# Last pair: turned output taken out ahead of f_down's product, residual ahead of two gate pairs; first round: next tile's rank product ahead of the turn

## The reference, cut to what matters

```python
x = L0_attn_x
xn = _layernorm(x, axis=-1)
s = _L0_attn_ref(xn, ...)         # RWKV-6: rank mix, r k v g w, state recurrence, group norm, gate, W_o
g = _silu(_L0_ffn_ref(xn, ...))   # silu(xn Wg) * (xn Wu), 2 of each 4 kept, times w_down (f_down)
x = x + s * g
xn = _layernorm(x, axis=-1)
s = _L1_attn_ref(xn, ...)         # Mamba-2 style: dt, B, C, X, scores in chunks of 32, states
g = _silu(_L1_ffn_ref(xn, ...))   # silu(xn Wg) * (xn Wu), times w_down (n_down)
x = x + s * g
# in _L0_attn_ref, the part that is moved:
xxx = x + xx * time_maa_x
a = jnp.tanh(xxx @ time_maa_w1).reshape(B, T, 5, D)
return yn * g @ W_o.T             # yn: normalised and scaled, turned to channels first by PE
```

## Time and profile before

| | us |
|---|---|
| median of three runs | 716.09 |
| lowest and highest | 715.89, 716.32 |
| the profiled execution | 717.52 |
| its span | 715.7 |
| PE busy with matmuls | 702.5 (98%) |
| DVE busy | 496.1 (69%) |
| ACT busy | 338.1 (47%) |
| POOL busy | 76.7 (11%) |

### The profile page before, as it was taken

One profiled execution on the slowest core, in us unless ns is written; L12 is line 12 of the kernel. 1 busy time (PEld: TensorE's weight loads), 2 busy tenths in 40 slices (PEclk: granted clock), 3 DMA queues, 4 the chain that ended last, 5 costly groups with the idle time before them and its releaser, 6 DMA issues.

```text
span 715.7 us, 18156 instructions
## 1 busy us (share of the span) xinstructions
PE 702.5 (98%) x7010; PEld 597.9 (84%) x7010; DVE 496.1 (69%) x1214; ACT 338.1 (47%) x671; POOL 76.7 (11%) x85
## 2 busy tenths in 40 slices
PE   7999999999999999999999999999999999999998
PEld 5777788888888788887888878888788888888887
DVE  5995988528884488755896568954789529895133
ACT  1423782147711586206852068421783237821790
POOL 6301011101110011100111001110011100110020
PEclk9999999999999999999999999999999999999999
DMA  7911460125501364012720236202370025601370
GB/s 231 408 44 30 136 103 18 22 82 143 96 2 30 102 128 83 16 30 89 149 61 16 52 120 110 47 15 74 104 128 23 16 77 136 105 12 25 122 120 16
DMA packets 139572, 59.46 MB, mean 83 GB/s; under 512 B 119728, under 2 KB 131312, under 8 KB 137968
## 3 DMA queue, kind: packets, MB, share of 16 engines
q1 hardware_dynamic: 139504, 58.44, 33.9%
HBM read 44.18 MB, written 14.24 MB: 82 GB/s over the span
## 4 chain that ended last, share of the span: by engine, by line
PE 87%; DVE 5%; issue 3%; DMA 2%; ACT 2%; SPq 1%; POOL 0%; DVEq 0%; POOLq 0%; ACTq 0%
PE psum L1542 68%; PE psum L1651 2%; PE psum L1763 2%; PE psum L1778 2%; ACT BC L626 1%; PE psum L1596 1%; PE psum L1621 1%; PE psum L1816 1%; PE psum L2002 1%; PE psum L1684 1%; PE psum L1863 1%; PE psum L1633 1%; PE psum L1789 1%; PE psum L1735 1%; PE psum L1724 1%
## 5 line engine op out<-in xcount | busy, mean ns | idle before, releaser
L626 ACT ACTIVATE BC<-psum 64x256 f32<-64x256 f32 x128 | 81.6, 637 | 1.9 <-PE psum L1542 0.2
L1542 PE MATMUL psum<-xn1T,sb_n_gate 128*128 128x256 f32 x256 | 61.3, 382 | 0.0
L1542 PE MATMUL psum<-xn1T,sb_n_up 128*128 128x256 f32 x256 | 60.5, 379 | 0.0
L1542 PE MATMUL psum<-xnT,sb_f_gate 128*128 128x256 f32 x240 | 57.8, 383 | 0.0
L1542 PE MATMUL psum<-xnT,sb_f_up 128*128 128x256 f32 x240 | 57.0, 379 | 0.0
L1542 PEld LDWEIGHTS psum<-xn1T,sb_n_gate 128*128 128x128 f32 x256 | 48.0, 190 | 6.8
L1542 PEld LDWEIGHTS psum<-xn1T,sb_n_up 128*128 128x128 f32 x256 | 48.2, 190 | 6.3
L757 ACT ACTIVATE thFB<-psum 128x512 f32<-128x512 f32 x8 | 4.8, 597 | 102.1 <-PE psum L1542 102.1
L1542 PEld LDWEIGHTS psum<-xnT,sb_f_up 128*128 128x128 f32 x240 | 45.2, 189 | 6.8 <-issue 0.3
L1542 PEld LDWEIGHTS psum<-xnT,sb_f_gate 128*128 128x128 f32 x240 | 44.7, 189 | 7.2 <-DVE xnT L1205 0.2
L1542 PE MATMUL psum<-sb_n_down,hidB 128*128 128x256 f32 x224 | 49.5, 379 | 0.0
(11 more groups left out here) (265 smaller groups left out, 1494.4 us busy)
## 6 DMA issues: line engine op xcount, KB each, us to landing
cs_row<-cs_dram SPq DMA_DIRECT2D x8, 1024.0 KB, 5.0
x_dram<-gate SPq DMA_DIRECT2D x8, 512.0 KB, 2.8
cs_half<-cs_dram SPq DMA_DIRECT2D x16, 256.0 KB, 5.8
hidB<-x_dram SPq DMA_DIRECT2D x8, 512.0 KB, 5.7
b_dram<-B_turned SPq DMA_DIRECT2D x32, 128.0 KB, 3.5
hidB<-b_dram SPq DMA_DIRECT2D x8, 512.0 KB, 4.2
X<-in_x SPq DMA_DIRECT2D x9, 256.0 KB, 2.9
XT<-in_x_turned SPq DMA_DIRECT2D x8, 256.0 KB, 2.9
```

The lines of the kernel that those rows point to most:

```text
L626: ins = a_.activation(cols[:, par, 2 * pair:2 * pair + 2, :], src[64 * par:64 * par + 64, :, s, :], ACT.Identity)
L1542: ins = t_.matmul(ps(t, name)[first_row:first_row + rows, col:col + n], w, x, start=(k == 0), stop=(k == len(ws) - 1))
```

## The change

In the last pair alone, ACT does `ffn_tanh(b, "n2", ...)`, `out_scaled` and `ffn_tanh_0` in this order, which were in the opposite order; DVE does `residual_0` ahead of `hidden_n(b, 2)` and `normed_1` ahead of `hidden_n(b, 3)`; PE does `out_0` ahead of `up_n(b, 2)`. At the end of the first round, DVE does `rank_inputs` ahead of `normed_1`, and PE the rank product of the next tile (`rank_first`, which was the first part of `rank_mix`) ahead of `turned_1`. In the first round `kept_busy` does 34 small products and not 39. At the start of PE's program, 40 instructions that only raise `passed` are put between the five identity products and the wait for the first tile.

```diff
@@ ACT, one(a, b), pairs @@
-                    ffn_tanh_0()
-                    out_scaled()
-                    ffn_tanh(b, "n2", thB[0], None, "n0")
+                    if a.reg is not None:
+                        ffn_tanh_0()
+                        out_scaled()
+                        ffn_tanh(b, "n2", thB[0], None, "n0")
+                    else:
+                        ffn_tanh(b, "n2", thB[0], None, "n0")
+                        out_scaled()
+                        ffn_tanh_0()
@@ DVE, one(a, b), pairs @@
-                    hidden_n(b, 2)
-                    residual_0()
-                    hidden_n(b, 3)
-                    normed_1()
+                    if a.reg is not None:
+                        hidden_n(b, 2)
+                        residual_0()
+                        hidden_n(b, 3)
+                        normed_1()
+                    else:
+                        residual_0()
+                        hidden_n(b, 2)
+                        normed_1()
+                        hidden_n(b, 3)
@@ DVE, one(a, b), first round @@
                     differences(a.next())
+                    rank_inputs(a.next())
                     normed_1()
-                    rank_inputs(a.next())
@@ PE @@
+                def rank_first(t):
+                    pe.wait_ge(xxx_ready, t.count(1, 1))
+                    loaded(t.first, "mix", 4)
+                    w1 = packed("w_mix1", NMIX * DMIX)
+                    open_bank(t, "a")
+                    for h in range(CH):
+                        t_.matmul(ps(t, "a")[:, 0:T], w1(h, 0, P), xxxT[:, h, :], start=(h == 0), stop=(h == CH - 1))
+
                 def rank_mix():
-                    pe.wait_ge(xxx_ready, a.count(1, 1))
-                    loaded(first_a, "mix", 4)
                     w1 = packed("w_mix1", NMIX * DMIX)
-                    open_bank(a, "a")
-                    for h in range(CH):
-                        t_.matmul(ps(a, "a")[:, 0:T], w1(h, 0, P), xxxT[:, h, :], start=(h == 0), stop=(h == CH - 1))
+                    if not first_b:
+                        rank_first(a)
@@ PE, last pair @@
                         close_bank(down_part(a, 1, 4, 8), a, "F0")
+                        out_0()
                         up_n(b, 2)
-                        out_0()
                         gate_n(b, 3)
@@ PE, first round @@
-                    kept_busy(["mix_w", "mix_k"], 39)
+                    kept_busy(["mix_w", "mix_k"], 34)
...
                     ffn_p(a.next(), 1)
+                    rank_first(a.next())
                     turned_1()
@@ PE, start @@
                 t_.matmul(ps(Tile(None, 0, first=True), "xT")[:, 0:T], ident[:, :], xnT[:, 0, 1:T + 1], start=True, stop=True)
+
+            for _ in range(40):
+                pe.sem_inc(passed, 1)
             pe.wait_ge(xn_ready, 1)
```

## The result

The changed kernel takes **720.53 us** (median of 4 runs, 718.03 to 721.72), the kernel before 716.21 in the same series (715.89 to 716.42): ratio 1.005, 95% interval 1.0029 to 1.0072. It is 4.3 us slower. The forecast was 716.7, in a range that ended at 718.9.

A forecast was written before the change was run, and what follows sets the result against it. PE, busy 98% of the span, was taken as the bound. +1.55 - 0.16 + 0 - 0.76 = +0.63 gave 718.15 on the profiled execution; the median, 1.43 lower, 716.7 us, range 715.0 to 718.9.

The forecast's parts named there:

- the cause that decided: Rival at the start: PE idles before the first turn and works on at half rate; +2.1 us, 718.8, chance 0.22.
- Steps: Start: 40 semaphore instructions at 0.150 us each delay the first tile's turn to 9.03; 1.55 us later, bounds 1.45 and 1.8.
- Small products: Start, first round: 5 fewer small products ahead of the rank product give 0.16 us back, bounds 0 and 0.16.
- Turn into the first pair: End of first round: idle is filled, but the rank product was already hidden beside ACT's copy; 0, bounds -0.1 and +0.2.
- Last pair: Last pair and step into the drain: out_0 waits less, the xn1T wait goes; 0.76 us back, bounds 0.5 and 0.95.
- Start: Start of PE's program: the 40 steps delay the turn and the whole first round by 1.55 us, none of it hidden.
- The rival's own test: Sign of the slow-start rival (chance 0.22): first half product takes over 1.5 us for its four passes.
- The rival's price: Slow start at half rate: half of a slow stretch of 4.6 us, less a little hidden; +2.1, 718.8, chance 0.22.
- The middle moves: Rival in six middle pairs: PE's instructions shift by 20 places; 0.2 us a pair, -1.2 or +1.2, chance 0.04 each way.

The follow-up runs named there:

- its own kernel: Kernel before with the last pair's three edits and nothing else; 716.71 us, ratio 0.999.
- the kernels with 0.37, 0.64 and 0.95: Seven identity products and 40 steps: on the kernel before, 732.01 us; on the changed kernel with 32 small products, 717.54; on the kernel before with 27, 717.86.
- the kernel with six identity products: Changed kernel with six identity products for five and 33 small products for 34, same instruction count; 719.35 us, ratio 1.0028.
- the 20-step version: Changed kernel with 20 steps for 40 and its small products back from 34 to 39, same instruction count; 715.77 us, ratio 0.9984.
- seven identity products: Changed kernel with seven identity products for five and 32 small products for 34, same instruction count; 717.54 us, ratio 1.0012.
- the kernel with seven products and 40 steps: Kernel before with the 40 steps and seven identity products for five, 48 more instructions; 732.01 us, ratio 1.0201.
- the kernel with 51 small products: Kernel before with 51 small products for 39 in the first round and nothing else, 48 more instructions; 728.8 us, ratio 1.0167.

## Why the prediction was wrong

It named the cause that decided and put it second, at 0.22 and with too small a price. Point by point:

- **Steps, +1.55: right.** First step at 2.8, last at 8.8, turn at 9.03. The Trainium skill (Advanced Engine Details and Errata, DMA Bandwidth Details) puts a semaphore increment at about one cycle; by that rule the turn would have stayed at 7.5. The rows decide against it for an increment that is an instruction of its own: 0.15 a step, 40 times.
- **Small products, -0.16: right in size at full rate**, 0.03 each: twelve fewer gave 0.35 (+1.07 to +0.72), twelve more cost 0.35. In the changed kernel itself the 34 ran at the lower clock, 2.11 where the 39 before took 1.36.
- **Turn into the first pair, 0: right** within its bounds, +0.13.
- **Last pair, -0.76: right**, 0.69 and 0.70 in two profiles, 0.6 in the median of its own kernel, by the steps that were given.
- **The failed step: "Start", that a delay of 1.55 costs 1.55.** The steps do not only delay the turn, they leave the array idle between the identity products and the turn. The forecast took the rate to be full from the first half product on, "as before", because 4.63 us of products come first in both. What stood in front was the same; what stood between was 1.65 us and not 0.10. After idles of 1.65 (twice), 1.72, 1.93 and 1.97 the half product's four passes took 1.82 to 2.08; after 0.16, 0.37, 0.64, 0.80 and 0.95, 1.13. The steps themselves and the late turn are not the cause, since the kernels with 0.37, 0.64 and 0.95 have both; nor does the length of the work ahead tell the two apart: behind 3.88 us of it and 0.80 of idle the passes were fast, behind 4.64 and 1.65 slow. The rival's own test, "over 1.5 us for its four passes", came out true.
- **The rival's price, +2.1:** it took half of one slow stretch of 4.6. By before's product at 20.14 the five slow profiles lay behind by 1.06, the delay as the traces have it, and by 1.3, 1.4 (the changed kernel's), 3.1, 4.2 and 4.2 more, and the two groups of the kernel with six identity products are 4.5 apart. The slow stretch ends earlier or later in each execution, up to past 18 us; a range that ended at 718.9 had room for the two mildest alone.
- **"The middle moves", 0.2 a pair:** not so for this kernel (+20), as the 20-step version shows. But its size was far off as a mechanism: +48 instructions cost 1 to 2 us in each pair. That the changed kernel was spared was luck; nothing in the forecast had priced what its position does.

The loss in three steps: the 20-step version is 0.9 under before; the delay brings it up by 1.77; and from seven identity products to the changed kernel itself the clock adds 3.2 (0.87 to 4.04 above before, across two series). That these make the measured +4.0 is no check, since each step is a difference of the same medians. The check is in the sizes: 1.77 beside 1.48 to 1.74 in the traces, and 3.2 between the 1.3 and 4.2 that the slow profiles lost to the clock.

What stays open: by what the position of the instructions acts. The page counts 57 packets of instructions in q8, 0.93 MB or 16 KB each, about one for every 256 of PE's 14,545 instructions, and the waits recur in each pair at the same two places. In the kernel with seven products and 40 steps no packet starts inside a wait, but one starts 1.1 to 1.9 us ahead of each of the 14 waits at line 1542, and PE goes on 2.2 to 2.9 us behind its start; in the kernel with 51 small products, all 14 again, 1.4 to 2.2 us ahead. A fetch of instructions that comes late would look so. It is likely and not shown: other packets have no wait behind them, in the kernel before too, and no run separated this from another cause. Also open is what happens to the clock between 0.95 and 1.65 us of idle, and whether the faster six executions of the kernel with six identity products had a shorter idle than the slower.

## What to carry to other kernels

A gap ahead of the first real product can cost more than its length, as 1.65 us did here and 0.95 did not: price it also with the work behind it at half rate, and shorten it or put array work into it (two more products won 3 us here). When a change adds or removes instructions ahead of a long unrolled stream, try it also with the count balanced elsewhere, since 48 that took 0.35 us themselves cost 12 us here and would be taken for the change's own. And list all executions with their times and clocks beside any profile: two groups in one kernel show the mechanism better than a median.

## What the runs showed of the hardware that was not expected

- After 1.65 to 1.97 us of idle behind 4.3 to 4.6 us of products, TensorE went at half rate for some 4 to 10 us in five profiles (granted clock 0.50 to 0.55 from 10.3 to 14.1 in four of them); after 0.95 or less it did not. One kernel did either, 6 executions to 6, 4.5 us apart.
- The Trainium skill (TensorE: Matmul & The Clock Gate, What's actually happening) has the slow rate as the default that activity lifts. The trace agrees, and adds that the lift is soon lost: in the changed kernel the turn at 9.03 ran at full rate (0.63), and the half product, 0.75 of idle later, at half (1.82).
- The granted clock column can miss it: in the kernel before with the 40 steps it read 1.00 where four passes took 2.08 and not 1.13. The length of a known product is the surer sign.
- With 48 more instructions in front of the pairs, 0.3% of the stream, TensorE had 14 waits of up to 1.6 us (13.2 us in one kernel, 8.5 in another) that it had not with the count balanced. Just ahead of each of them, by 1.1 to 2.2 us, a packet of the instruction queue starts.
